# Expert outputs written to zeroed rows for first and second choice instead of being added by scatters

## The reference, cut to what matters

```python
def _L0_ffn_ref(x, router_w, router_b, experts_inter, experts_out):
    cap = math.ceil(n_tok / n_exp * CAPACITY_FACTOR)          # 4096 / 8 = 512
    logits = jnp.einsum('bsh,eh->bse', x, router_w) + router_b
    weights_flat = jax.nn.softmax(logits, axis=-1).reshape(n_tok, n_exp)
    topk_vals, topk_idx = jax.lax.top_k(weights_flat, TOP_K)  # the two best of 8
    ...
    sorted_indices = jnp.argsort(-expert_mask, axis=0)[:cap]  # first 512 tokens of each expert
    ...
    h = jax.nn.relu(jnp.einsum('ceh,ehi->cei', inputs, experts_inter))
    out = jnp.einsum('cei,eih->ceh', h, experts_out) * in_w[..., None]
    combined = jnp.zeros_like(x_flat).at[used_idx].add(out.reshape(-1, hidden))
    combined = combined + x_flat * (noop_w * noop_mask)[:, None]
    return combined.reshape(batch, seq, hidden)
...
x = x + 0.5 * _L0_ffn_ref(_layernorm(x, axis=-1), ...)
x = x + _L0_attn_ref(...)
x = x + 0.5 * _L0_ffn_ref(_layernorm(x, axis=-1), ...)
```

## Time and profile before

| | |
|---|---|
| median of 3 runs | 2966.94 us |
| the profiled execution | 2966.22 us, its span 2964.5 us |
| first run of the stage | 44 to 208.9 us of the span |
| second run of the stage | 314.5 to 479 us |
| PE, DVE, ACT, POOL busy over the span | 79%, 68%, 63%, 33% |

### The profile page before, as it was taken

The page is one execution under the profiler, slowest core; times in us unless marked ns, Lnnn a source line. Parts: engine busy times, 40 slices in busy tenths (PEclk is TensorE's granted clock), DMA queues, the critical chain, the costliest instruction groups (busy, mean ns, idle before and its releaser), DMA issues. The chain is left out here.

```text
span 2964.5 us, 44016 instructions
## 1 busy us (share of the span) xinstructions
PE 2356.5 (79%) x13097; PEld 1220.5 (41%) x13097; DVE 2009.4 (68%) x5780; ACT 1861.4 (63%) x4759; POOL 974.5 (33%) x1296
## 2 busy tenths in 40 slices
PE   4647484738888878499999999997858888888887
PEld 4425453512222246244444444444524444444452
DVE  4616633759899947566666666665568999998854
ACT  2124223327777763377777777776539999999964
POOL 2553275344353332400000000003644444444436
PEclk8778596559999985799999999999769999999979
DMA  6330232023223200000000000000011111111001
GB/s 173 78 53 1 89 69 39 0 42 75 53 49 77 51 8 1 30 1 1 1 1 1 1 1 1 1 1 1 1 34 30 29 30 30 29 30 30 1 1 29
DMA packets 230444, 86.76 MB, mean 29 GB/s; under 512 B 175362, under 2 KB 223298, under 8 KB 230210
## 3 DMA queue, kind: packets, MB, share of 16 engines
q1 hardware_dynamic: 215104, 74.74, 10.8%
q0 software_dynamic: 9856, 7.58, 1.8%
q10 hardware_dynamic: 5250, 1.62, 0.3%
HBM read 26.47 MB, written 15.50 MB: 14 GB/s over the span
## 5 line engine op out<-in xcount | busy, mean ns | idle before, releaser
L2375 ACT ACTIVATE s_pT<-s_ps_t 128x512 f32<-128x512 f32 x1024 | 625.1, 638 | 139.7 <-PE s_ps_t L1975 123.9
L2128 DVE TENSOR_REDUCE s_neg_max<-s_ps_a 128x1 f32<-128x512 f32 x1024 | 666.1, 682 | 63.0 <-PE s_ps_a L1941 53.0
L2366 ACT ACTIVATE s_first<-s_ps_a,s_neg_max 128x512 f32<-128x512 f32 x512 | 390.5, 763 | 25.1 <-DVE s_neg_max L2128 23.4
L2784 ACT ACTIVATE s_e<-s_e,s_neg_max 128x128 f32<-128x128 f32 (+3 forms) x512 | 283.2, 555 | 165.6 <-DVE s_neg_max L2684 163.3
L1987 PE MATMUL s_ps_t<-ident,s_first 128*128 128x128 f32 x2048 | 316.1, 285 | 83.8 <-ACT s_pT L2375 71.3
L2297 POOL TENSOR_SCALAR s_first<-s_first,s_rec 128x512 f32<-128x512 f32 x128 | 232.3, 1815 | 365.6 <-DVE s_rec L2134 359.6
L2684 DVE CUSTOM_DVE_ANT_0 s_e<-s_ps_a,w_alibi 128x128 f32<-128x128 f32 (+3 forms) x512 | 230.7, 487 | 110.9 <-PE s_ps_a L2554 109.9
L1941 PE MATMUL s_ps_a<-s_lanesT 64*128 64x512 bf16 x1024 | 275.2, 401 | 37.3 <-DMA s_lanesT<-n_lanes 20.4
L1987 PEld LDWEIGHTS s_ps_t<-ident,s_first 128*128 128x128 f32 x2048 | 220.8, 141 | 183.5 <-ACT s_pT L2375 141.5
L2002 PE MATMUL s_ps_o<-s_pT,n_v_pad 128*32 128x512 f32 x2048 | 275.9, 612 | 12.2 <-ACT s_oT L2381 12.2
L139 POOL TENSOR_TENSOR s_rstd<-s_ve,minus_half 128x4 f32<-128x4 f32 x24 | 26.4, 1099 | 678.8 <-DVE s_ve L126 678.2
(11 more groups left out here) (382 smaller groups left out, 4079.7 us busy)
## 6 DMA issues: line engine op xcount, KB each, us to landing
s_token_rows<-s_rows SPq DMA_DIRECT2D x4, 1088.0 KB, 5.4
s_x_rows<-x SPq DMA_DIRECT2D x4, 1024.0 KB
x<-s_x_rows SPq DMA_DIRECT2D x8, 512.0 KB, 6.1
s_Wi<-L_ffn_experts_inter SPq DMA_DIRECT2D x2, 1792.0 KB, 8.0
x<-L_attn_x SPq DMA_DIRECT2D x4, 512.0 KB, 7.9
out<-x SPq DMA_DIRECT2D x4, 512.0 KB, 5.3
s_lanesT<-n_lanes SPq DMA_TRANSPOSE x64, 4.1
s_shiftedT<-n_lanes SPq DMA_TRANSPOSE x64, 2.4
```

The source lines that it names most:

```text
L2128: dve.tensor_reduce(neg_max[:, column(n):column(n) + 1], sa[n % NA][:], AX.X, ALU.max, negate=True).then_inc(s.max_ready, 1)
L2366: act.activation(first[:, g % NF, n % PU, :], sa[n % NA][:], ACT.Exp, bias=neg_max[:, n:n + 1], accum_out=sum1[:, n % (NR * PU):n % (NR * ...
L2375: act.activation(pT[:, n % NP, :], st[n % NK][:], ACT.Exp).then_inc(s.probs_ready, 1)
L2784: act.activation(part, part, ACT.Exp, bias=neg_max[:, n:n + 1], scale=-1.0, accum_out=total[:, n:n + 1]).then_inc(s.first_ready, 1)
```

## The change

The results are no longer added in HBM. Each of the two runs of the stage gets `y_rows`, two sets of rows, one for the first and one for the second choice. SP fills the token rows of both with zeros near the stage's start, by 16 DMAs of 256 KB (4 MB) from a zeroed tile, where before 2.25 MB of x were stored. `scatter(e)` writes without adding. No two experts share a row now, so only the DMA of the same quarter of `scatter(e-1)` is waited for. To know the choice, DVE puts 64 more in the tile number of a second choice (`told_tile`), and `read_slots` makes a second list (`to_index`). `keep_own` moves into the expert loop, five or six tiles behind each `weigh` but the first. At the end SP loads both sets, eight DMAs of 512 KB through four buffers, and DVE adds them to x, eight times 128 by 1024 (`add_rows`).

The semaphores are now taken from a common pool with the lowest numbers first. That touches every stage's barrier, and nothing else in the other stages.

```diff
+        numbers = [h.num for h in s]
+    nc.all_engine_barrier(sems_to_clear=range(min(numbers), max(numbers) + 1))
...
                 sp.wait_ge(s.empty_set, 1)
                 sp.dma_start(by_tile(token_rows)[:, NT:, :], empty[:]).then_inc(s.empty_stored, 16)
+                for c in range(2):
+                    for b in range(B):
+                        sp.dma_start(by_tile(y_rows[c * ROWS:(c + 1) * ROWS])[:, b * TB:(b + 1) * TB, :],
+                                     zeros[:, b % 2].rearrange("p (t d) -> p t d", d=D)).then_inc(s.y_cleared, 16)
...
-                for h in range(HALVES):
-                    sp.wait_ge(s.x_ready, WT * (h + 1))
-                    sp.dma_start(by_tile(x_rows)[:, half(h), :], G.x[:, half(h), :]).then_inc(s.x_stored, 16)
...
                 for q in range(Q):
                     sp.wait_ge(scattered[q], 16 * E)
+                for n in range(2 * B // 2):
+                    c, i = n % 2, n // 2
+                    if n >= 4:
+                        sp.wait_ge(s.x_added, n - 3)
+                    sp.dma_start(parts[:, n % 4].rearrange("p (t d) -> p t d", d=D),
+                                 by_tile(y_rows[c * ROWS:(c + 1) * ROWS])[:, 2 * TB * i:2 * TB * (i + 1), :]).then_inc(loaded[n % 4], 16)
-                for i in range(4):
-                    tiles = slice(i * NT // 4, (i + 1) * NT // 4)
-                    sp.dma_start(G.x[:, tiles, :], by_tile(x_rows)[:, tiles, :]).then_inc(s.x_loaded, 16)
...
+                def add_rows(n):
+                    i = n // 2
+                    if n == 0:
+                        dve.wait_ge(s.x_kept, NT)
+                    if n % 2:
+                        dve.wait_ge(s.x_added, n)
+                    x = G.x[:, 2 * TB * i:2 * TB * (i + 1)].rearrange("p t d -> p (t d)")
+                    dve.wait_ge(loaded[n % 4], 16 * (n // 4 + 1))
+                    dve.tensor_tensor(x, x, parts[:, n % 4], ALU.add).then_inc(s.x_added, 1)
...
+                    do(dve.scalar_tensor_tensor(out=told_tile[:], in0=second[:], scalar=float(SECOND),
+                                                in1=tile_no[:].unsqueeze(2).to_broadcast([P, NT, KINDS]),
+                                                op0=ALU.mult, op1=ALU.add))
...
+                    do(dve.tensor_scalar(is_second[:], slots[:, 0], float(SECOND), None, ALU.is_gt))
-                    do(dve.scalar_tensor_tensor(out=index[:, e, :], in0=row[:], scalar=float(-P), in1=none[:],
+                    do(dve.scalar_tensor_tensor(out=row[:], in0=row[:], scalar=float(-P), in1=none[:],
                                                 op0=ALU.add, op1=ALU.add))
+                    do(dve.scalar_tensor_tensor(out=index[:, e, :], in0=is_second[:], scalar=float(-P * SECOND), in1=row[:],
+                                                op0=ALU.mult, op1=ALU.add))
                     dve.engine_nop().then_inc(s.index_ready, 1)
+                    dve.scalar_tensor_tensor(out=to_index[:, e, :], in0=is_second[:], scalar=float(ROWS - P * SECOND), in1=row[:],
+                                             op0=ALU.mult, op1=ALU.add).then_inc(s.to_index_ready, 1)
...
-                keep_own(0)
-                keep_own(1)
+                do(dve.tensor_copy(noop[:], rows[:, :, D + E]))
                 for e in range(E):
                     if e + 3 < E:
                         mark(e + 3)
                     if e + 2 < E:
                         read_slots(e + 2)
                     weigh(e)
+                    if e:
+                        for t in range((e - 1) * NT // (E - 1), e * NT // (E - 1)):
+                            keep_own(t)
+                for n in range(B):
+                    add_rows(n)
...
                 def scatter(e):
                     pool.wait_ge(s.y_ready, e + 1)
-                    if e:
-                        for q in range(Q):
-                            pool.wait_ge(scattered[q], 16 * e)
-                    for q in range(Q):
-                        at = bass.IndirectOffsetOnAxis(ap=index[:, e, q:q + 1], axis=0)
-                        pool.indirect_dma_start(out=x_rows, out_offset=at, in_=y[:, e % 2, q, :], in_offset=None,
-                                                compute_op=ALU.add).then_inc(scattered[q], 16)
+                    pool.wait_ge(s.to_index_ready, e + 1)
+                    for q in range(Q):
+                        if e:
+                            pool.wait_ge(scattered[q], 16 * e)
+                        at = bass.IndirectOffsetOnAxis(ap=to_index[:, e, q:q + 1], axis=0)
+                        pool.indirect_dma_start(out=y_rows, out_offset=at, in_=y[:, e % 2, q, :], in_offset=None
+                                                ).then_inc(scattered[q], 16)
...
-                pool.memset(empty[:], 0.0).then_inc(s.empty_set, 1)
+                do.free(pool.memset(empty[:], 0.0))
+                do(pool.memset(zeros[:], 0.0))
+                pool.engine_nop().then_inc(s.empty_set, 1)
```

More of the change, by code:

```diff
@@ L62, in semaphores, with lasting, clear @@
 def semaphores(nc, names):
-    for n in names.split():
-        if n not in ALL_SEMS.made:
-            ALL_SEMS.made[n] = ALL_SEMS.ctx.enter_context(nc.semaphore(n))
-    return namedtuple("Semaphores", names)(*[ALL_SEMS.made[n] for n in names.split()])
-def clear(nc, s):
-    cleared = range(min(h.num for h in s), max(h.num for h in s) + 1)
-    assert set(cleared) <= {h.num for h in ALL_SEMS.made.values()}
-    nc.all_engine_barrier(sems_to_clear=cleared)
+    names = names.split()
+    while len(ALL_SEMS.free) < len(names):
+        ALL_SEMS.made += 1
+        ALL_SEMS.free.append(ALL_SEMS.ctx.enter_context(nc.semaphore(f"stage{ALL_SEMS.made}")))
+    taken, ALL_SEMS.free = ALL_SEMS.free[:len(names)], ALL_SEMS.free[len(names):]
+    return namedtuple("Semaphores", names)(*taken)
+def lasting(nc, names):
+    made = namedtuple("Lasting", names)(*[ALL_SEMS.ctx.enter_context(nc.semaphore(n)) for n in names.split()])
+    assert not ALL_SEMS.made and not ALL_SEMS.lasting
+    ALL_SEMS.lasting = made
+    return made
+def clear(nc, s, last=False):
+    numbers = [h.num for h in s]
+    assert not set(numbers) & {h.num for h in ALL_SEMS.free}
+    assert min(numbers) > max([h.num for h in ALL_SEMS.lasting], default=-1)
+    if last:
+        numbers += [h.num for h in ALL_SEMS.lasting]
+    nc.all_engine_barrier(sems_to_clear=range(min(numbers), max(numbers) + 1))
+    ALL_SEMS.free = sorted([*s, *ALL_SEMS.free], key=lambda h: h.num)
 NORM_SEMS = "v_chain g_chain a_chain p_chain var_ready rstd_ready xn_ready xnT_psum xnT_ready "
@@ L692, in capacity_experts_ffn @@
         m, r, noop = sb("m", [P, NT]), sb("r", [P, NT]), sb("noop", [P, NT])
-        T = RankTiles(rest=sb("rest", [P, WT, KINDS])[:], top=sb("top", [P, WT])[:], desc=G.desc[:])
+        top = sb("top", [P, WT])
         tile_no, token_no, quarter_no, empty_row = (sb(n, [P, w]) for n, w in (
@@ L702, in capacity_experts_ffn @@
         slots, row, none = sb("slots", [P, 2, Q]), sb("row", [P, Q]), sb("none", [P, Q])
-        index = sb("index", [P, E, Q], I32)
+        index, to_index = (sb(n, [P, E, Q], I32) for n in ("index", "to_index"))
+        second, told_tile = sb("second", [P, NT, KINDS]), sb("told_tile", [P, NT, KINDS])
+        is_second, zeros, parts = sb("is_second", [P, Q]), sb("zeros", [P, 2, TB * D]), sb("parts", [P, 4, TB * D * 2])
         Wi, Wo = sb("Wi", [D, E, I]), sb("Wo", [P, E, C, D])
@@ L833, in choose @@
                     do(dve.tensor_tensor(probs[:, at], probs[:, at], r[:, at].unsqueeze(2).to_broadcast(wide), ALU.mult))
+                    T = RankTiles(rest=second[:, at], top=top[:], desc=G.desc[:])
                     top2_mask(do, dve, T, probs[:, at], mask[:, at], WT)
@@ L840, in choose, with keep_own @@
                     dve.engine_nop().then_inc(s.rows_ready, 1)
-                def keep_own(h):
-                    do(dve.tensor_copy(noop[:, half(h)], rows[:, half(h), D + E]))
-                    for t in range(h * WT, (h + 1) * WT):
-                        dve.scalar_tensor_tensor(out=G.x[:, t, :], in0=xn[:, t, :], scalar=noop[:, t:t + 1],
-                                                 in1=G.x[:, t, :], op0=ALU.mult, op1=ALU.add).then_inc(s.x_ready, 1)
+                def keep_own(t):
+                    dve.scalar_tensor_tensor(out=G.x[:, t, :], in0=xn[:, t, :], scalar=noop[:, t:t + 1],
+                                             in1=G.x[:, t, :], op0=ALU.mult, op1=ALU.add).then_inc(s.x_kept, 1)
+                def add_rows(n):
[7 more added lines that the diff above has]
+                    dve.tensor_tensor(x, x, parts[:, n % 4], ALU.add).then_inc(s.x_added, 1)
                 def number():
@@ L2858, in program @@
     with ExitStack() as ctx:
-        ALL_SEMS.ctx, ALL_SEMS.made = ctx, {}
+        ALL_SEMS.ctx, ALL_SEMS.made, ALL_SEMS.free, ALL_SEMS.lasting = ctx, 0, [], ()
         G = setup(nc, ctx, inp)
```

20 lines of the change are left out of this document (12 added, 8 removed).

## The result

| | median of the runs | lowest to highest |
|---|---|---|
| before | 2966.57 us (4 runs) | 2965.95 to 2968.70 |
| after | 2948.49 us (4 runs) | 2946.11 to 2951.80 |

The ratio is 0.9939, 95% interval 0.9921 to 0.9956: the change makes the kernel 18 us faster. 2965 was forecast, with a range down to 2955. The profiled execution of after took 2948.37 us, its span is 2946.7.

A forecast was written before the change was run, and what follows sets the result against it. GpSimd's queue was taken as the bound, then the compute chain. Per run, -9.1 and -9.2 us in the expert loop against +8.3 at the end gave -1.7 together: 2966.2 to 2964.5, 2965 for the median; range 2955 to 2976.

The forecast's parts named there:

- The scatter's price: GpSimd's issue of a scatter without the add would cost what a gather does, 0.96 us instead of 1.56.
- The first index: Three extra VectorE instructions ahead of the first index would delay GpSimd and TensorE by 0.86 us.
- Gather 2: In the expert loop, GpSimd's gather for expert 2 would start at 114.6 instead of 113.30.
- The two marks behind the copies: In the expert loop, marks 5 and 6 queued behind `keep_own` on VectorE would cost twice 0.2 us, +0.4.
- Issues held up by VectorE: Pieces of `keep_own` among GpSimd's issues would hold these up by 1.5 us in all, costing nothing in the sum.
- From the last weighing to the loads: After the last result: 0.2 us to start, 4.7 for the last scatter's issues, 1.74 to SP's loads, at 189.3.
- The tail: At the stage's end, doubled loads would add 7.0 us and the last add 1.25: +8.3 us per run.
- The zeroing and the stores behind it: Near the stage's start, zeroing 4.2 MB and the token-row stores would stay hidden, with ten us before the first gather.
- "So the compute chain becomes the bound, and the gain is cut off there": In the expert loop, GpSimd would be done at 177, but the last result only at 182.67: -9.1 us to the loads.
- the "-0.56" for gather 6: The last expert's beat of 10.33 us would lose its wait for that gather and become 9.77: -0.56 us.
- "the compute chain was itself slowed": Rival: the pause at expert 3 and the long next beat would go, up to 5.4 us more per run; chance 0.15.

The follow-up runs named there:

- a_order: The changed kernel with the copies between the experts moved ahead of the weighing instead of behind it: 2946.8 us, ratio 0.9936.
- a_one: The changed kernel loading and adding only the first choices' set of result rows, so its output leaves out the second choices: 2933.2 us, ratio 0.9885.
- a_add_again: The changed kernel with the add put back into its scatters: 2979.0 us at first, 2977.4 us when repeated on another chip.
- a_slow_again: The changed kernel, scatters still plain, with a 128x320 memset on GpSimd ahead of each scatter: 2965.7 us at first, 2963.3 us when repeated on another chip.
- a_room: The changed kernel with an unused tile of 2,560 bytes per partition: 2980.3 us at first, 2946.6 us when repeated on another chip.
- b_plain: The kernel before with plain instead of adding scatters, its output leaving out the sums: 2964.1 us at first, 2931.2 us when repeated on another chip.
- groups A and C: Two sets of follow-up kernels, each run on one chip beside before (2970.3 and 2971.6 us); every profiled kernel there had expert-loop pauses of 2 to 5 us.
- a_best: a_order with the result rows in partition order, so loads read 4 KB stretches instead of 512-byte rows: 2974.4 us at first, 2944.4 us when repeated on another chip.
- after_again: The changed kernel run once more, word for word, in a later group on another chip: 2947.3 us, ratio 0.9928.

## Why the prediction was wrong

**The scatter's price** (0.96 us from the gather's row): right, 0.97.

**The first index** (+0.86): right. From the stage's first instruction on VectorE to the first gather it is 52.39 us, before it was 51.51. **Gather 2** came 0.5 us earlier than forecast, at 114.07 for 114.6.

**The two marks behind the copies** (+0.4): right, 0.19 + 0.25 us by the beats of after against those of a_order.

**Issues held up by VectorE** (1.5 us taken): issues from gather 2 to scatter 6 ran 2.9 us over their usual length (2.3 in before). It cost nothing in itself, as was said.

**From the last weighing to the loads** (7.3 us): right, 180.89 - 173.66 = 7.23.

**The tail** (+8.3): right within 0.3 us, 8.52 in the profile; 7.5 of it by a_one is the second set of rows.

**The zeroing and the stores behind it** (hidden): the first gather came no later than by VectorE's terms, so nothing came through. Doubling the zeroing to find the edge of the cover wasn't tried.

**"So the compute chain becomes the bound, and the gain is cut off there": this is the step that failed**, with the last result at 182.67 where it was at 173.66 + 0.69 = 174.35. That is 8.3 us per run, 16.6 in both, and the forecast missed by 16.5. The sentence on which it rested, that the last result "was only there at 181.97", took the weighings of the earlier trace rows as the chain's own beat. They weren't. I had GpSimd's row at 12.5 us per expert, against a chain that needs 9.35; and yet I priced the row by its end alone, and forgot that the gathers on which the chain lives stand in it, behind the scatters of earlier experts. A row that is longer than the chain's beat delays the chain as soon as its lead of two experts is spent. Experiments a_add_again and a_slow_again show it.

It stood in the trace of before. Its row has no gap over 0.31 us from gather 2 at 113.30 to the end of scatter 4 at 177.64, and the last quarter of the last gather, issued in it at 169.16, is what TensorE waits for:

```profile
169.16 0.94 POOL L994 DMA_INDIRECT s_xg<-s_token_rows,s_index  x1 [0.30 <-issue]
...
171.68 0.33 PE L773 MATMUL s_ps_xT<-ident,s_xg 128*128 128x128 f32 x1 [0.98 <-DMA s_xg<-s_token_rows,s_index]
```

From there to the last weighing, at 181.28, it is the chain's 9.6 us. The second run shows the same, with 0.78 us of waiting and 9.65 us. So the "-0.56" for gather 6 was the right mechanism at a wrong price: the wait seen is 1 us long, but what the row sets is the time at which the last expert can begin.

In after the row takes 4 x 1.26 + 4 x 1.27 = 10.1 us an expert by the medians, and 10.2 to 11.1 from one gather to the next in the timeline. That is still over the beat, and the lead just lasts: the last quarter of gather 6 is issued at 161.03 and, with the 2.6 us that a gather takes (median), there at 163.6, less than 1 us before TensorE turns it.

**The pause at expert 3, and the rival that named it.** In the profiled execution of before, the beats to the weighings of experts 3 and 4 are 3.5 and 2.3 us longer than after's, by a pause like those of a_room (weighing and copy both some 3 us behind TensorE's rows, released by something "remote"). After has none. The rival "the compute chain was itself slowed" thus named the right sign, with a chance of 0.15. But the pause did not set the end of before's loop. GpSimd's row ran on through it without a gap, so without the pause TensorE would only have waited longer for gathers 5 and 6. a_add_again bears this out: it has the adds and no pause, and takes 65.4 us from the first weighing to the last; before takes 65.1, after 56.9. The rival also took "gathers and adding scatters alternate" only as a coincidence of time, where the order of GpSimd's row makes it a cause. The two delays lie on top of each other: both had to go for the gain that was measured. With the adds gone and stalls still there, the kernel before gains only 6 us (b_plain, 2964.1 for 2970.3).

**What stays open.** What makes the pauses, and whether the one in before's trace came with the chip of that execution or with the kernel: the records don't name that chip.

**How far the result holds.** On the chips of groups A and C a kernel with after's loop stalls. a_room, which elsewhere runs as after does, is slower than before there: 1.0029 (1.0019 to 1.0040) for 0.9923. The kernels whose GpSimd row is the bound hardly care: a_slow 2965.7 and 2963.3, a_add 2979.0 and 2977.4, and before 2970 to 2972 for 2967 to 2969. Those with room in it lose 30 us and more: b_plain 2964.1 for 2931.2, a_best 2974.4 for 2944.4. After itself had no run on such a chip, so that it too is slower than before there is inferred from a_room.

## What to carry to other kernels

When one engine issues both what feeds a chain and what drains it, its row counts at every step: add up its issues per step, and if the sum is more than the chain's beat, the times seen in the chain can be the row's and not the chain's. Before taking a beat as an engine's own, look at what that engine waits for, the last time above all: a pause earlier in the chain can hide a wait that would take its place. And when two kernels that should run alike differ, run one of them again on the other's chip before building a theory on it.

## What the hardware showed that was not expected

- An adding scatter of 128 rows takes GpSimd 1.56 us to issue, a plain one 0.97, a gather 0.96; 0.30 lie between two. By the queue's 9,856 and 3,584 packets for 56 gathers and 56 scatters, an adding scatter makes 112 packets more than a plain one: 144 for 32, if a gather and a plain scatter make equally many.
- Loads of 512-byte rows run at 289 to 311 GB/s with the stream full (after, after_again), of 4 KB at 369 to 393 (a_best_again, 182 to 188). The Trainium skill ("DMA: Bandwidth & Descriptors", section "Where 436 GB/s comes from") gives about 358 GB/s for one core; the trace is above that. The Trainium skill ("Perfetto Trace Analysis", section "Roofline") says that a single active core can pull more than that share, and the trace of this kernel, which runs on one core, agrees with its 393 GB/s.
- The same program takes 2946.6 us on one chip and 2980.3 on another, by pauses of 2 to 5 us between TensorE's last matmul and the two engines that wait for it. a_room has them at the same experts in both runs of the stage, and its ten executions lie between 2975.9 and 2986.7.
- TensorE's clock fell to half behind such a pause (a_room) and behind waits for gathers (a_add_again), and stayed at full through all the beats of after (1.00 from 112 to 175).
